# One buffer for the outer weights of both halves of a convolution, filled pair by pair from DRAM in each half image

## The chip, the core and the metric

The kernel runs on one core of a Trainium2 chip. The time is the device time of one execution in microseconds (us); the number compared is the median of the runs. The core has a matrix engine (TensorE, PE in the profile), a vector engine (VectorE, DVE), a scalar engine (ScalarE, ACT), a general engine (GpSimd, POOL) and a sync engine (SyncE, SP), which here only issues transfers. All five run their own instruction streams and meet at semaphores. Sixteen DMA engines move data between DRAM and the on-chip memory; SP, ACT and POOL each have a queue to them.

## What is computed

The reference takes `x` of shape (32, 256, 28, 28) in float32, averages it over 12 log-polar bins of a 9x9 window, convolves the 12 averages with `w_conv1` (256x256x4x3), adds a 1x1 convolution and a bias, normalises each channel over the whole batch, adds `x`, and clips at zero:

```
xp = log_pooling(x)                              # 12 bin averages for each pixel
out = conv(xp, w_conv1, stride=(4, 3)) + conv(x, w_center) + b_center
out = (out - mean) * rsqrt(var + EPS)            # mean, var over batch, height, width
out = out * gamma + beta
return relu(out + x)
```

The batch statistics need every image before the first output can be written, so the work has two phases.

## The kernel before, in words

**Phase 1** goes over 32 images, and in each over the two halves `c` of the 256 input channels, 128 channels a half. A half image has the number `s = 2 * image + c`, 0 to 63. For each half image VectorE builds sums and differences of shifted copies of `x` (helped by two accumulating transfers a half from POOL, `row2`, which the profile calls `row`, and `ends`), ScalarE and VectorE split them into a high and a low part (`inner_split`, `pooled_split`), and TensorE multiplies them with weights that are split in the same way: three matmuls (lines 888 to 890) for each product. The weights have 16 taps. Ten are inner taps (`w_first` for half 0, `w_inner` for half 1); six are outer taps, `w_first_outer` for half 0 and `w_outer` for half 1, each 128 x 3072 float32. The outer taps are used in three pairs `j`, 24 matmuls each; the inner part of a half image is 60 matmuls. TensorE adds to `pooled_done` after each pair (line 946) and to `inner_done` after the inner part (line 929).

**The order on SP** (`image_steps`, line 382) is one load of `x` for each half image, for the next image, which waits for three sums of VectorE and ScalarE, and one store of the previous image's result `y` to `y_dram` for each image.

**Phase 2**, called the tail here, reads `y` and `x` of all 32 images again, scales and clips them and writes the output. It uses the memory of phase 1 as 31 places of 784 KB (1568 columns); place `k` holds the `y` (even `k`) or the `x` (odd `k`) of the tail's image slots 1 to 15. Most places are filled while phase 1 is still running, as soon as what lay there has been used for the last time. SP fills place 1 before the next to last image's steps, and places 2 to 8 behind them, with `load_places(2, 9)`. Then come (lines 427 to 441) `load_places(9, AFTER_STAGE)` with `AFTER_STAGE` 10, `load_places(AFTER_STAGE, AFTER_FIRST_INNER)` with 13 after the last but one half image's inner part, `load_places(AFTER_FIRST_INNER, AFTER_FIRST)` with 15 after its third pair, and the rest as the last half image goes on. Sixteen images are in flight at a time, two rounds in all; in the second round every load waits for a store of the first.

Of the kernel before, what the change touches and what calls it, by code (L numbers as in the profile page):

```python
# [6 lines left out]

def conv_bn_relu_program(nc, x, x_wide, w_raw, w_side, b_center, gamma, beta, out, y_dram):
    F32 = mybir.dt.float32
    F32R = mybir.dt.float32r  # L10
# [9 lines left out]
    CHANNELS = P * CH  # L20
# [50 lines left out]
    with ctx:  # L71
# [11 lines left out]
        with ExitStack() as phase1:  # L83
            def reused(name, size, dt=F32):
                size = -(-size // 8) * 8
                start_of[name] = used[0]
                used[0] += size
                end_of[name] = used[0]
                return phase1.enter_context(nc.sbuf_tensor(name, [P, size], dt))

            w_stage = reused("w_stage", CH * RAW * CHANNELS)

            spare = reused("spare", 10 * CH * HW - CH * RAW * CHANNELS)
            w_first = reused("w_first", 2 * INNER_TAPS * CHANNELS, F32R)
            w_first_outer = reused("w_first_outer", 2 * (TAPS - INNER_TAPS) * CHANNELS, F32R)

            d03 = reused("d03", ROW3_H * (W + 3) + EDGES)
            row2 = reused("row2", (W + 3) * ROW2_H)
            ends = reused("ends", W * ENDS_H)
            INNER = 6 * HALF  # L100
            inner_split = reused("inner_split", 2 * INNER, F32R)
            w_inner = reused("w_inner", 2 * INNER_TAPS * CHANNELS, F32R)
            pooled_split = reused("pooled_split", PAIRS * 2 * PAIR, F32R)
            w_outer = reused("w_outer", 2 * (TAPS - INNER_TAPS) * CHANNELS, F32R)

# [33 lines left out]

        def w_part(c, lo, tap):  # L140

            if tap < INNER_TAPS:
                return (w_first, w_inner)[c], (lo * INNER_TAPS + tap) * CHANNELS
            return (w_first_outer, w_outer)[c], (lo * (TAPS - INNER_TAPS) + tap - INNER_TAPS) * CHANNELS

# [10 lines left out]
        def outer_weights(c, g):  # L156

            a, b = (t - INNER_TAPS for t in GROUPS[g][:2])
            n = (1, (b - a) * CHANNELS)
            split = (w_first_outer, w_outer)[c]  # L160
            return (view(split, a * CHANNELS, n),
                    view(split, (TAPS - INNER_TAPS + a) * CHANNELS, n),
                    view(spare, ((25, 6)[c] + a) * CHANNELS, n))
# [14 lines left out]

        AFTER_STAGE = places_within("spare")
        AFTER_FIRST_INNER = places_within("w_first")  # L180
        AFTER_FIRST = places_within("w_first_outer")
        AFTER_SUMS = places_within("ends")
# [49 lines left out]
        w_hi_ready = sem("w_hi_ready")  # L232
        w_lo_ready = sem("w_lo_ready")
        w_outer_hi_ready = sem("w_outer_hi_ready")
        w_outer_begun = sem("w_outer_begun")
# [132 lines left out]
        def _(sp):  # L368
# [10 lines left out]

            def image_steps(image, first=False, last=False):  # L380
# [71 lines left out]
        def _(act):  # L452
            def split_weights(c, groups):
                for g in groups:
                    a, b, raw, factor = GROUPS[g]
                    if raw is None:
                        act.wait_ge(w_sums_ready, c + 1)
                        source = w_sums(c, 0, b - a)
                    else:
                        act.wait_ge(w_loaded[c][raw >= RAW_OUTER], 16)  # L460
                        source = view(w_stage, (c * RAW + raw) * CHANNELS, (1, (b - a) * CHANNELS))
                    dst, at = w_part(c, 0, a)
                    nc.scalar.activation(view(dst, at, (1, (b - a) * CHANNELS)), source, ACT.Copy,
                                         scale=factor).then_inc(w_hi_ready, 1)
# [159 lines left out]
        def _(dve):  # L624
# [36 lines left out]
            def lo_of_weights(c, groups):  # L661
                for g in groups:
                    a, b, raw, factor = GROUPS[g]
                    dve.wait_ge(w_hi_ready, c * (len(GROUPS) - 1) + g + 1)
                    if raw is None:
                        source = w_sums(c, 0, b - a)
                    else:
                        source = view(w_stage, (c * RAW + raw) * CHANNELS, (1, (b - a) * CHANNELS))
                    hi, hi_at = w_part(c, 0, a)
                    lo, lo_at = w_part(c, 1, a)  # L670
# [210 lines left out]
        def _(pe):  # L881
            def products(c, o, tap, place, buf, hi, lo, *dims, start=False, stop=False):

                hi_w, hi_at = w_part(c, 0, tap)
                lo_w, lo_at = w_part(c, 1, tap)
# [12 lines left out]

            with pe.Fori(0, IMAGES) as image:
                for c in range(CH):  # L900
                    s = CH * image + c
                    pe.wait_ge(w_lo_ready, c * (len(GROUPS) - 1) + M_GROUP)
                    pe.wait_ge(inner_lo_ready, 2 * s + 1)
# [12 lines left out]
                    if c == CH - 1:  # L916
                        last.then_inc(m_done, 1)
                    pe.wait_ge(w_lo_ready, c * (len(GROUPS) - 1) + INNER_GROUPS)
                    pe.wait_ge(inner_lo_ready, 2 * s + 2)
# [10 lines left out]
                    for j in range(PAIRS):  # L930
                        if c == j == 0:
                            pe.wait_ge(w_lo_ready, FIRST_OUTER_GROUP)
                        elif j < 2:
                            pe.wait_ge(w_outer_lo_ready[2 * c + j - 1], 16)
                        pe.wait_ge(pooled_lo_ready, PAIRS * s + j + 1)
                        u, h = PAIR_SHAPE[j]
                        for m, (u0, h0) in enumerate(PAIR_PLACES[j]):
                            for o in range(CH):
                                for q in range(2):
                                    place = view(acc, (2 * o + q) * BANK + u0 * H + h0, (H, u), (1, h))  # L940

                                    between, step = (HALF_PLANE, h) if j == 2 else (h, 2 * h)
                                    at = 2 * j * PAIR + m * PAIR // 2 + q * between
                                    last = products(c, o, TAP_OUTER + 2 * j + m, place, pooled_split, at, at + PAIR,
                                                    (step, u), (1, h), stop=c == CH - 1 and j == PAIRS - 1 and m == 1)
                        last.then_inc(pooled_done, 1)


# [46 lines left out]
```

## Time and profile before

| | us |
|---|---|
| median of 3 runs | 1601.26 (1601.02 to 1601.95) |
| the profiled execution's own time | 1600.99 |
| its span | 1599.3 |
| PE busy | 1456.9 |
| DVE busy | 1467.5 |
| ACT busy | 770.1 |
| POOL busy | 129.5 |

The span is what the profiler records, from the first to the last instruction; 1.7 us of the execution's time lie around it. TensorE works from the start to 1460.7 us, and the tail takes the rest. DVE's sum is the larger one because DVE works in the tail too.

### The profile page before, as it was taken

To read this page: it belongs to the slowest core of one execution; us is meant where nothing else is said; L and a number is where in the kernel's file an instruction comes from. 1 tells how busy PE (TensorE), PEld (TensorE's weight loads), DVE (VectorE), ACT (ScalarE), POOL (GpSimd) and SP (SyncE) were. 2 spreads that over 40 slices of the span, in tenths; PEclk is the share of its full clock that TensorE was granted. 3 is DMA by queue.
4 is the path that set the end of the run, shared out by engine and by line. 5 is a ranking of instruction groups with operands and counts; after the bars stand their busy time and mean duration, and the time that the engine had idled before them with its cause. 6 is when DMAs were issued, how large, how long until landed. Compare 5 with 4: busy or idle time off the path is not lost.

```text
span 1599.3 us, 22801 instructions
## 1 busy us (share of the span) xinstructions
PE 1456.9 (91%) x8518; PEld 1455.7 (91%) x8518; DVE 1467.5 (92%) x1500; ACT 770.1 (48%) x863; POOL 129.5 (8%) x165
## 2 busy tenths in 40 slices
PE   9999999999999999999999999999999999995000
PEld 9999999999999999999999999999999999995000
DVE  8999999999999999999999999999999999996731
ACT  6554454544444454445444554445444554444632
POOL 2100000000000000000000000000000000000100
PEclk9999999999999999999999999999999999998555
DMA  8544444334434444344434444344434444569999
GB/s 219 100 120 91 74 85 94 77 85 90 88 77 86 74 85 91 76 89 86 88 77 90 74 85 87 78 92 85 86 78 86 81 85 105 161 193 383 416 425 402
DMA packets 47721, 201.65 MB, mean 126 GB/s; under 512 B 5664, under 2 KB 5664, under 8 KB 47712
## 3 DMA queue, kind: packets, MB, share of 16 engines
q0 software_dynamic: 21824, 86.55, 29.9%
q1 hardware_dynamic: 21024, 89.32, 15.4%
q10 hardware_dynamic: 4864, 25.69, 3.9%
q14 instruction: 7, 0.06, 0.0%
q8 instruction: 2, 0.03, 0.0%
HBM read 148.85 MB, written 49.77 MB: 124 GB/s over the span
## 4 chain that ended last, share of the span: by engine, by line
PE 88%; ACT 4%; ACTq 3%; DVE 3%; issue 1%; DMA 0%; DVEq 0%
PE acc L888 29%; PE acc L890 29%; PE acc L889 29%; ACTq L620 3%; ACT phase L617 2%; ACT phase_rest L617 2%; DVE phase_rest L625 1%; DVE pooled_split L626 0%; ACT unread L554 0%; DVE d L625 0%; ACT x_pad L617 0%; DVE inner_split L626 0%; DMA x_pad<-x 0%; DVE w_first L671 0%; DVE w_inner L671 0%
## 5 line engine op out<-in xcount | busy, mean ns | idle before, releaser
L501 ACT ACTIVATE pooled_split<-phase_rest 128x1456 fp32r<-128x1456 f32 x192 | 273.7, 1425 | 581.0 <-DVE phase_rest L625 581.0
L626 DVE TENSOR_TENSOR pooled_split<-phase_rest,pooled_split 128x1456 fp32r<-128x1456 f32 x192 | 318.0, 1671 | 0.0
L888 PE MATMUL acc<-pooled_split,w_first_outer 128*128 128x364 f32 x768 | 253.7, 330 | 0.3 <-DVE pooled_split L626 0.3
L888 PE MATMUL acc<-pooled_split,w_outer 128*128 128x364 f32 x768 | 252.1, 328 | 0.8 <-DVE pooled_split L626 0.8
L890 PE MATMUL acc<-pooled_split,w_outer 128*128 128x364 f32 x768 | 252.8, 329 | 0.0
L889 PE MATMUL acc<-pooled_split,w_outer 128*128 128x364 f32 x768 | 252.5, 329 | 0.0
L889 PE MATMUL acc<-pooled_split,w_first_outer 128*128 128x364 f32 x768 | 252.5, 329 | 0.0
L890 PE MATMUL acc<-pooled_split,w_first_outer 128*128 128x364 f32 x768 | 252.3, 329 | 0.0
L888 PE MATMUL acc<-inner_split,w_inner 128*128 128x392 f32 (+1 forms) x640 | 215.8, 337 | 1.3 <-DVE w_inner L671 1.3
L888 PE MATMUL acc<-inner_split,w_first 128*128 128x392 f32 (+1 forms) x640 | 216.7, 339 | 0.0
L889 PE MATMUL acc<-inner_split,w_inner 128*128 128x392 f32 (+1 forms) x640 | 216.6, 338 | 0.0
L890 PE MATMUL acc<-inner_split,w_inner 128*128 128x392 f32 (+1 forms) x640 | 216.6, 338 | 0.0
L890 PE MATMUL acc<-inner_split,w_first 128*128 128x392 f32 (+1 forms) x640 | 215.9, 337 | 0.0
L889 PE MATMUL acc<-inner_split,w_first 128*128 128x392 f32 (+1 forms) x640 | 215.4, 337 | 0.0
L480 ACT ACTIVATE inner_split<-phase_rest 128x1568 fp32r<-128x1568 f32 x64 | 97.5, 1524 | 127.5 <-DVE phase_rest L625 127.5
L888 PEld LDWEIGHTS acc<-pooled_split,w_outer 128*128 128x128 f32 x768 | 144.2, 188 | 1.1 <-DVE pooled_split L626 1.1
L888 PEld LDWEIGHTS acc<-pooled_split,w_first_outer 128*128 128x128 f32 x768 | 144.4, 188 | 0.6 <-DVE pooled_split L626 0.6
L889 PEld LDWEIGHTS acc<-pooled_split,w_outer 128*128 128x128 f32 x768 | 144.5, 188 | 0.0
L889 PEld LDWEIGHTS acc<-pooled_split,w_first_outer 128*128 128x128 f32 x768 | 144.5, 188 | 0.0
L890 PEld LDWEIGHTS acc<-pooled_split,w_first_outer 128*128 128x128 f32 x768 | 144.4, 188 | 0.0
L890 PEld LDWEIGHTS acc<-pooled_split,w_outer 128*128 128x128 f32 x768 | 144.4, 188 | 0.0
L305 POOL DMA_DIRECT2D row<-x_wide x64 | 56.2, 878 | 1039.3 <-ACT row L490 1019.0
(110 smaller groups left out, 2493.2 us busy)
## 6 DMA issues: line engine op xcount, KB each, us to landing
row<-x_wide POOLq DMA_DIRECT2D x64, 558.0 KB, 5.8
ends<-x_wide POOLq DMA_DIRECT2D x64, 504.0 KB, 5.5
x_pad<-x SPq DMA_DIRECT2D x64, 392.0 KB, 3.1
y_dram<-y_stage SPq DMA_DIRECT2D x30, 784.0 KB, 3.3
out<-phase ACTq DMA_DIRECT2D x16, 784.0 KB, 28.2
phase<-y_dram SPq DMA_DIRECT2D x15, 784.0 KB, 15.3
phase_rest<-y_dram SPq DMA_DIRECT2D x14, 784.0 KB, 13.4
out<-phase_rest ACTq DMA_DIRECT2D x14, 784.0 KB, 29.8
```

Source lines behind the costliest of these rows:

```text
L305: return pool.dma_start(view(buf, 0, (1, n_columns * TALL_PITCH)), x_wide[bass.ds(image, 1), :, c, bass.ds((first_column + EDGE) * TALL_PI ...
L480: nc.scalar.activation(view(inner_split, 0, (1, SD)), reused_view(INNER_LOW, (1, SD)), ACT.Copy)\
L501: nc.scalar.activation(view(pooled_split, 2 * j * PAIR, (1, PAIR)), reused_view(POOLED_LOW + 2 * j * PAIR, (1, PAIR)), ACT.Copy)\
L617: nc.scalar.activation(x_slot(d, o), x_slot(d, o), ACT.Relu, bias=bn_shift[:, o:o + 1]).then_inc(relu_done, 1)
L620: act.dma_start(out[tail_image(round_, d)].rearrange("p c w h -> p c (w h)"), x_slot_whole(d)).then_inc(stored[d], 16)
L625: add = lambda out_, a, b: nc.vector.tensor_tensor(out_, a, b, ALU.add)
L626: sub = lambda out_, a, b: nc.vector.tensor_tensor(out_, a, b, ALU.subtract)
L888: nc.tensor.matmul(place, hi_w, hi_in, start=start, stop=False)
L889: nc.tensor.matmul(place, lo_w, hi_in, start=False, stop=False)
L890: return nc.tensor.matmul(place, hi_w, lo_in, start=False, stop=stop)
```

## The change

The two buffers for the outer weights become one, `w_outer`. Half 0's outer weights are made in it; half 1's are made in a new buffer `w_made` that lies ahead of `w_first` in memory and is used by image 0 alone. Once both are made, SP stores them to a new DRAM tensor `w_dram`. From half image 3 on, each pair's weights (both parts, 128 x 2 x 512 float32, 512 KB) are loaded into their third of `w_outer` when the same pair of the half image before is done. TensorE's first image is written out ahead of its loop, since it reads other buffers.

```
-            w_first_outer = reused("w_first_outer", 2 * (TAPS - INNER_TAPS) * CHANNELS, F32R)
+            spare = reused("spare", 12 * CH * HW - CH * RAW * CHANNELS - 2 * (TAPS - INNER_TAPS) * CHANNELS)
+            w_made = reused("w_made", 2 * (TAPS - INNER_TAPS) * CHANNELS, F32R)
...
-        AFTER_STAGE = places_within("spare")
+        AFTER_STAGE = places_within("w_made")
         AFTER_FIRST_INNER = places_within("w_first")
-        AFTER_FIRST = places_within("w_first_outer")
...
+            def save_outer_weights():
+                sp.wait_ge(w_lo_ready, FIRST_OUTER_GROUP)
+                sp.wait_ge(w_outer_lo_ready[0], 16)
+                for c in range(CH):
+                    if c == 1:
+                        for k in range(1, 3):
+                            sp.wait_ge(w_outer_lo_ready[k], 16)
...
+                    sp.dma_start(w_dram[c].rearrange("p l f -> p (l f)"), ...).then_inc(w_saved, 16)
+                sp.wait_ge(w_saved, CH * 16)
+
+            def load_outer_weights(s, c, j):
+                sp.wait_ge(pooled_done, PAIRS * s - PAIRS + j + 1)
+                dst, src = outer_of_pair(c, j)
+                sp.dma_start(dst, src).then_inc(w_outer_loaded[j], 16)
...
+                    change = not first and not (second and c == 0)
+                    if change:
+                        load_outer_weights(s, c, 0)
+                        load_outer_weights(s, c, 1)
                     if not last:
                         sp.wait_ge(row3_ready, CH * image + c + 1)
                         sp.wait_ge(v_ready, CH * image + c + 1)
                         sp.wait_ge(ends_begun, CH * image + c + 1)
                         load_x(image + 1, c)
+                    if change:
+                        load_outer_weights(s, c, 2)
                     if c == 0 and not first and not last:
+                        if second:
+                            sp.wait_ge(first_added, 32)
                         sp.wait_ge(y_ready, CH * image + FREE)
...
             image_steps(0, first=True)
-            sp.wait_ge(first_added, 32)
-            with sp.Fori(1, LAST - 2) as image:
+            save_outer_weights()
+            image_steps(1, second=True)
+            with sp.Fori(2, LAST - 2) as image:
                 image_steps(image)
...
             sp.wait_ge(inner_done, CH * IMAGES - 1)
             load_places(AFTER_STAGE, AFTER_FIRST_INNER)
-            sp.wait_ge(pooled_done, PAIRS * (CH * IMAGES - 1))
-            load_places(AFTER_FIRST_INNER, AFTER_FIRST)
             sp.wait_ge(inner_lo_ready, 2 * CH * IMAGES)
             sp.wait_ge(pooled_ready, PAIRS * CH * IMAGES)
-            load_places(AFTER_FIRST, AFTER_SUMS)
+            load_places(AFTER_FIRST_INNER, AFTER_SUMS)
...
-            with pe.Fori(0, IMAGES) as image:
+            def image_steps(image, first=False):
                 for c in range(CH):
                     s = CH * image + c
-                    pe.wait_ge(w_lo_ready, c * (len(GROUPS) - 1) + M_GROUP)
+                    if first:
+                        pe.wait_ge(w_lo_ready, c * (len(GROUPS) - 1) + M_GROUP)
...
                     for j in range(PAIRS):
-                        if c == j == 0:
+                        if not first:
+                            pe.wait_ge(w_outer_loaded[j], 16 * (s - 1))
+                        elif c == j == 0:
                             pe.wait_ge(w_lo_ready, FIRST_OUTER_GROUP)
...
+            image_steps(0, first=True)
+            for j in range(PAIRS):
+                pe.sem_inc(w_outer_loaded[j], 16)
+            with pe.Fori(1, IMAGES) as image:
+                image_steps(image)
```

SP's queue in the main loop, half 0 of an image, before: the load of `x` behind its three waits, and the store of `y`.

```order
13 L370 ISA [waits ends_begun,v_ready,row3_ready]
14 L370 DMA x_pad<-x 128x784
15 L389 ISA [waits y_ready]
16 L389 DMA y_dram<-y_stage 128x1568
17 L383 REGISTER_ALU
```

The same place now:

```order
20 L408 DMA w_outer<-w_dram 128x2x512 [waits pooled_done]
21 L406 REGISTER_ALU
22 L408 DMA w_outer<-w_dram 128x2x512 [waits pooled_done]
23 L419 REGISTER_ALU
24 L376 ISA [waits ends_begun,v_ready,row3_ready]
25 L376 DMA x_pad<-x 128x784
26 L408 DMA w_outer<-w_dram 128x2x512 [waits pooled_done]
27 L429 ISA [waits y_ready]
28 L429 DMA y_dram<-y_stage 128x1568
```

Two loads of weights, each behind a count of TensorE's pairs, have come ahead of the load of `x`, and a third between it and the store of `y`.

SP's queue at the end of phase 1, before, from place 8 on (`phase` is the memory of the tail's first places; `y_dram` rows fill even places, `x` rows odd ones):

```order
35 L393 DMA phase<-y_dram 128x1568
36 L396 DMA phase<-x 128x1568 [waits y_saved]
37 L393 DMA phase<-y_dram 128x1568 [waits inner_done]
38 L396 DMA phase<-x 128x1568
39 L393 DMA phase<-y_dram 128x1568
40 L396 DMA phase<-x 128x1568 [waits pooled_done]
41 L393 DMA phase<-y_dram 128x1568
42 L396 DMA phase<-x 128x1568 [waits pooled_ready,inner_lo_ready]
```

The same place now, from place 8 on:

```order
60 L433 DMA phase2<-y_dram 128x1568
61 L408 DMA w_outer<-w_dram 128x2x512 [waits pooled_done] x6
62 L436 DMA phase2<-x 128x1568 [waits y_saved]
63 L433 DMA phase2<-y_dram 128x1568
64 L436 DMA phase2<-x 128x1568
65 L433 DMA phase2<-y_dram 128x1568 [waits inner_done]
66 L436 DMA phase2<-x 128x1568
67 L433 DMA phase2<-y_dram 128x1568
68 L436 DMA phase2<-x 128x1568 [waits pooled_ready,inner_lo_ready]
```

Six loads of weights, those of the last two half images, now stand between place 8 and place 9 (row 62). Places 9, 10 and 11 have no wait of TensorE's own any more, 12, 13 and 14 wait for `inner_done`, and all of them come behind row 61.

## Rows read from the trace of the kernel before

**Rows 1.** The page: busy time by engine, and the DMA rate in 40 slices.

```profile
PE 1456.9 (91%) x8518; PEld 1455.7 (91%) x8518; DVE 1467.5 (92%) x1500; ACT 770.1 (48%) x863; POOL 129.5 (8%) x165
...
GB/s 219 100 120 91 74 85 94 77 85 90 88 77 86 74 85 91 76 89 86 88 77 90 74 85 87 78 92 85 86 78 86 81 85 105 161 193 383 416 425 402
```

**Rows 2.** Windows of three half images: stretch, busy by engine, clock, DMA share, GB/s.

```profile
51.34:73.88 22.54, 22.54 (x132) 22.54 (x133) 20.81 (x22) 13.22 (x14) 4.13 (x5) 1.00 0.50 89
795.01:817.55 22.54, 22.54 (x133) 22.54 (x133) 22.02 (x22) 13.64 (x18) 2.60 (x3) 1.00 0.42 78
1426.10:1448.65 22.55, 22.55 (x134) 22.55 (x133) 22.37 (x22) 11.93 (x15) 0.87 (x1) 1.00 0.83 265
```

**Rows 3.** PE in order of time around 795 us: start, duration, instruction.

```profile
794.83 0.34 PE L890 MATMUL acc<-inner_split,w_first 128*128 128x392 f32 x1
795.01 0.33 PE L888 MATMUL acc<-pooled_split,w_first_outer 128*128 128x364 f32 x1
...
807.01 0.34 PE L888 MATMUL acc<-inner_split,w_inner 128*128 128x392 f32 x1
...
817.57 0.33 PE L888 MATMUL acc<-pooled_split,w_outer 128*128 128x364 f32 x1
```

**Rows 4.** SP in order of time, 795 to 845 us.

```profile
803.34 22.96 SPq L370 DMA_DIRECT2D x_pad<-x  x2
831.77 0.36 SPq L389 DMA_DIRECT2D y_dram<-y_stage  x1
```

**Rows 5.** The page's DMA issues: count, size of one, median us to landing.

```profile
row<-x_wide POOLq DMA_DIRECT2D x64, 558.0 KB, 5.8
...
x_pad<-x SPq DMA_DIRECT2D x64, 392.0 KB, 3.1
```

**Rows 6.** DMA issues from 1389 to 1412 us.

```profile
row<-x_wide POOLq DMA_DIRECT2D x1, 558.0 KB, 9.6
```

**Rows 7.** POOL in order of time: a start transfer, two in phase 1.

```profile
42.48 0.87 POOL L339 DMA_DIRECT2D w_outer<-spare  x1 [9.47 <-ACT w_outer L476]
...
836.52 0.87 POOL L305 DMA_DIRECT2D row<-x_wide  x1 [19.63 <-ACT row L490]
...
1397.48 0.87 POOL L305 DMA_DIRECT2D row<-x_wide  x1 [14.80 <-ACT row L490]
```

**Rows 8.** DVE in order of time: the first readers of those two sums.

```profile
847.25 0.97 DVE L625 TENSOR_TENSOR d<-row,x_pad 128x840 f32<-128x840 f32 x1
...
1410.69 0.97 DVE L625 TENSOR_TENSOR d<-row,x_pad 128x840 f32<-128x840 f32 x1
```

**Rows 9.** SP in order of time at the end of phase 1.

```profile
1392.84 0.45 SPq L396 DMA_DIRECT2D phase<-x  x1
1426.13 0.33 SPq L393 DMA_DIRECT2D phase<-y_dram  x1
...
1427.09 0.46 SPq L393 DMA_DIRECT2D phase<-y_dram  x1
1438.13 0.33 SPq L396 DMA_DIRECT2D phase<-x  x1
...
1448.70 0.33 SPq L396 DMA_DIRECT2D phase_rest<-x  x1
```

**Rows 10.** Windows from the end of phase 1 to the tail.

```profile
1415.00:1422.00 7.00, 7.00 (x42) 7.00 (x41) 6.45 (x6) 2.77 (x3) 0.00 (x0) 1.00 0.00 0
1439.00:1440.00 1.00, 1.00 (x7) 1.00 (x7) 1.00 (x2) 0.77 (x1) 0.00 (x0) 1.00 0.82 107
1439.00:1460.70 21.70, 21.63 (x127) 21.34 (x126) 10.08 (x10) 5.71 (x5) 0.00 (x0) 1.00 0.92 345
1455.00:1460.00 5.00, 5.00 (x33) 5.00 (x32) 0.00 (x0) 0.00 (x0) 0.00 (x0) 1.00 1.01 424
...
1472.00:1490.00 18.00, 0.00 (x0) 0.00 (x0) 18.00 (x21) 14.02 (x17) 2.38 (x4) 0.50 1.02 403
1490.00:1580.00 90.00, 0.00 (x0) 0.00 (x0) 40.89 (x43) 40.98 (x47) 6.37 (x12) 0.50 1.02 425
```

More of the change, by code:

```diff
@@ L5, with conv_bn_relu_program @@
 from concourse import mybir
-def conv_bn_relu_program(nc, x, x_wide, w_raw, w_side, b_center, gamma, beta, out, y_dram):
+def conv_bn_relu_program(nc, x, x_wide, w_raw, w_side, b_center, gamma, beta, out, y_dram, w_dram):
     F32 = mybir.dt.float32
@@ L91, in conv_bn_relu_program @@
             w_stage = reused("w_stage", CH * RAW * CHANNELS)
-            spare = reused("spare", 10 * CH * HW - CH * RAW * CHANNELS)
+            spare = reused("spare", 12 * CH * HW - CH * RAW * CHANNELS - 2 * (TAPS - INNER_TAPS) * CHANNELS)
+            w_made = reused("w_made", 2 * (TAPS - INNER_TAPS) * CHANNELS, F32R)
             w_first = reused("w_first", 2 * INNER_TAPS * CHANNELS, F32R)
-            w_first_outer = reused("w_first_outer", 2 * (TAPS - INNER_TAPS) * CHANNELS, F32R)
             d03 = reused("d03", ROW3_H * (W + 3) + EDGES)
@@ L138, in row3v_edges, with w_part @@
             return row3v(-ROW3V_AT, (ROW3V_H, W + 3), (1, EDGES))
-        def w_part(c, lo, tap):
+        OUTER_TAPS = TAPS - INNER_TAPS
+        def w_part(c, lo, tap, made=False):
             if tap < INNER_TAPS:
                 return (w_first, w_inner)[c], (lo * INNER_TAPS + tap) * CHANNELS
-            return (w_first_outer, w_outer)[c], (lo * (TAPS - INNER_TAPS) + tap - INNER_TAPS) * CHANNELS
+            at = (lo * OUTER_TAPS + tap - INNER_TAPS) * CHANNELS
+            if made and c == 1:
+                return w_made, at
+            return w_outer, at
         def w_sums(c, first, n):
@@ L159, in outer_weights @@
             n = (1, (b - a) * CHANNELS)
-            split = (w_first_outer, w_outer)[c]
-            return (view(split, a * CHANNELS, n),
-                    view(split, (TAPS - INNER_TAPS + a) * CHANNELS, n),
+            (high, high_at), (low, low_at) = (w_part(c, lo, a + INNER_TAPS, made=True) for lo in range(2))
+            return (view(high, high_at, n), view(low, low_at, n),
                     view(spare, ((25, 6)[c] + a) * CHANNELS, n))
@@ L233, in conv_bn_relu_program @@
         w_lo_ready = sem("w_lo_ready")
+        w_saved = sem("w_saved")
+        w_outer_loaded = [sem(f"w_outer_loaded{j}") for j in range(PAIRS)]
         w_outer_hi_ready = sem("w_outer_hi_ready")
@@ L378, in load_weights, with outer_of_pair, image_steps @@
                     .then_inc(w_loaded[c][part], 16)
-            def image_steps(image, first=False, last=False):
-                for c in range(CH):
+            def outer_of_pair(c, j):
+                n = 2 * CHANNELS
+                return (view(w_outer, j * n, (OUTER_TAPS * CHANNELS, 2), (1, n)).bitcast(F32),
+                        w_dram[c, :, :, j * n:(j + 1) * n])
+            def save_outer_weights():
+                sp.wait_ge(w_lo_ready, FIRST_OUTER_GROUP)
+                sp.wait_ge(w_outer_lo_ready[0], 16)
+                for c in range(CH):
+                    if c == 1:
+                        for k in range(1, 3):
+                            sp.wait_ge(w_outer_lo_ready[k], 16)
+                    made, made_at = w_part(c, 0, INNER_TAPS, made=True)
+                    sp.dma_start(w_dram[c].rearrange("p l f -> p (l f)"),
+                                 view(made, made_at, (1, 2 * OUTER_TAPS * CHANNELS)).bitcast(F32)).then_inc(w_saved, 16)
+                sp.wait_ge(w_saved, CH * 16)
[3 more added lines that the diff above has]
+                sp.dma_start(dst, src).then_inc(w_outer_loaded[j], 16)
+            def image_steps(image, first=False, second=False, last=False):
+                for c in range(CH):
+                    s = CH * image + c
+                    change = not first and not (second and c == 0)
+                    if change:
+                        load_outer_weights(s, c, 0)
+                        load_outer_weights(s, c, 1)
                     if not last:
@@ L461, in split_weights @@
                         source = view(w_stage, (c * RAW + raw) * CHANNELS, (1, (b - a) * CHANNELS))
-                    dst, at = w_part(c, 0, a)
+                    dst, at = w_part(c, 0, a, made=True)
                     nc.scalar.activation(view(dst, at, (1, (b - a) * CHANNELS)), source, ACT.Copy,
@@ L668, in lo_of_weights @@
                         source = view(w_stage, (c * RAW + raw) * CHANNELS, (1, (b - a) * CHANNELS))
-                    hi, hi_at = w_part(c, 0, a)
-                    lo, lo_at = w_part(c, 1, a)
+                    hi, hi_at = w_part(c, 0, a, made=True)
+                    lo, lo_at = w_part(c, 1, a, made=True)
                     nc.vector.scalar_tensor_tensor(
@@ L881, in _, with products @@
         def _(pe):
-            def products(c, o, tap, place, buf, hi, lo, *dims, start=False, stop=False):
-                hi_w, hi_at = w_part(c, 0, tap)
-                lo_w, lo_at = w_part(c, 1, tap)
+            def products(c, o, tap, place, buf, hi, lo, *dims, start=False, stop=False, made=False):
+                hi_w, hi_at = w_part(c, 0, tap, made)
+                lo_w, lo_at = w_part(c, 1, tap, made)
                 hi_w, lo_w = (view(w, at + o * P, (1, P)) for w, at in ((hi_w, hi_at), (lo_w, lo_at)))
@@ L917, in _ @@
                         last.then_inc(m_done, 1)
-                    pe.wait_ge(w_lo_ready, c * (len(GROUPS) - 1) + INNER_GROUPS)
+                    if first:
+                        pe.wait_ge(w_lo_ready, c * (len(GROUPS) - 1) + INNER_GROUPS)
                     pe.wait_ge(inner_lo_ready, 2 * s + 2)
@@ L944, in _ @@
                                     last = products(c, o, TAP_OUTER + 2 * j + m, place, pooled_split, at, at + PAIR,
-                                                    (step, u), (1, h), stop=c == CH - 1 and j == PAIRS - 1 and m == 1)
+                                                    (step, u), (1, h), stop=c == CH - 1 and j == PAIRS - 1 and m == 1,
+                                                    made=first)
                         last.then_inc(pooled_done, 1)
+            image_steps(0, first=True)
[3 more added lines that the diff above has]
+                image_steps(image)
 def kernel(x, L0_conv_w_conv1, L0_conv_w_center, L0_conv_b_center, L0_conv_gamma, L0_conv_beta):
@@ L990 @@
     y_dram = nc.dram_tensor("y_dram", (images, 128, halves * height * width), f32, kind="Internal").ap()
-    conv_bn_relu_program(nc, *args, out, y_dram)
+    w_dram = nc.dram_tensor("w_dram", (halves, 128, 2, 6 * channels), f32, kind="Internal").ap()
+    conv_bn_relu_program(nc, *args, out, y_dram, w_dram)
     result = run_bass_kernel_spmd(nc, [arrays], core_ids=[0])
```

## The prediction, made before the changed kernel was run

> **What bounds the kernel now.** I read the page's busy shares first, then windows of single half images, then the engines in order of time, and last windows of the end. The page shows TensorE busy for 91% of the span and the DMA rate at 74 to 120 GB/s until late, then near 400 [rows 1]. The windows make two regimes of it. In phase 1 TensorE has no gap: a half image takes 22.54 us, and TensorE is busy for all 22.54 of them at full clock, from 51.34 us on [rows 2]. VectorE is busy for 22.02 of a middle half image, so it has 0.5 us to spare. From 1460.70 us TensorE has nothing to do, and the DMA engines are busy all the time, at 425 GB/s from 1490 to 1580 us [rows 10]. So phase 1 is bound by TensorE and the tail by the bytes that have not been moved when it begins. A change counts if it opens a gap on TensorE, or if it changes how many bytes are still to be moved.
>
> **Part 1, the memory.** Does one buffer less make room? No. Before, the 1568-column places are cut from 48,632 columns: stage and spare 15,680, `w_first` 5120, `w_first_outer` 3072, the three sum buffers 3128, `inner_split` 4704, `w_inner` 5120, `pooled_split` 8736, `w_outer` 3072. Now stage, spare and `w_made` take 18,816 and the rest 29,880, in all 48,696. Both give 31 places. The tail has the same 16 slots, two rounds and bytes. What moves is when a place is free: `AFTER_STAGE` goes from 10 to 12, `AFTER_FIRST_INNER` from 13 to 15.
>
> **Part 2, the reloads in phase 1.** Half images 3 to 63 load three pairs each, 183 loads of 0.524 MB, 95.9 MB. Per half image that is 1.57 MB, or 70 GB/s over 22.54 us, on top of 78 [rows 2]; together 148 against the 424 that pure loads reach [rows 10].
>
> Is a reload in time? The pairs run from 795.01 to 807.01 us, so one takes 4.0 us, and the next half image's pair 0 starts at 817.57 [rows 3]. Pair 0's third is free at 799.0 and wanted at 817.57, which leaves 18.6 us; the other two pairs have the same. No trace row shows a 512 KB reload. The nearest are the 392 KB load of `x` with 3.1 us and, as the slow end, a 558 KB accumulating transfer under a full queue with 9.6 us [rows 5, 6]. I take 3.5 us, by the nearer one; even 9.6 is 9 us below what there is. Cost 0.
>
> Does SP get to them? It now waits for pair 1 before the load of `x`. Pair 1 ends at 803.0, the load of `x` goes out at 803.34 anyway, and the second one at 803.34 + 22.96, that is 826.3, behind the pair 1 that ends at 817.57 + 8 = 825.6 [rows 3, 4]. What is queued behind the wait is delayed by a DMA issue of some 0.4 us, and that `x` is read only in the next image's sums. Pair 2's load follows at 807.0 and 829.6, the store of `y` at 831.77 as before. Cost 0.
>
> Do the loads slow others? The tightest neighbour is `row`, the accumulating sum. It is issued at 836.52, lands 5.8 us later, and VectorE reads it at 847.25, so 4.9 us are spare [rows 5, 7, 8]. The reloads would go out near 821.6, 825.6, 829.6 and 844.2, none within those 5.8 us. `ends` has more room. Under a full queue `row` took 9.6 us, from 1397.48 to 1407.1, and was read at 1410.69 with no wait [rows 6 to 8]. And TensorE ran a half image in 22.55 us with the DMA engines 83% busy [rows 2]. Cost 0; if the cover is gone, see the third rival.
>
> TensorE's own waits: leaving out the waits for results, a half image had four waits for weights against constants (two of them in the inner part), now three against a register, one ahead of each pair. The step into pair 0, with two waits, costs 795.01 - 794.83 = 0.18 us from start to start, and the mean step of the inner part is (817.57 - 807.01) / 60 = 0.176 us, so a wait that is already met is worth next to nothing [rows 3]. Bounds: 0.01 us a half image either way, 0.6 us in all. I take 0.
>
> **Part 3, the start.** Two stores of 1.57 MB (3.7 us each at 425 GB/s) leave SP from 43 us on, behind the load of `x` for image 1. The low outer weights, issued at 42.48 [rows 7], share the engines with the first. They are wanted by pair 1 of half image 1, at 51.34 + 4 = 55.3 us [rows 2]. With the 5.8 to 9.6 us of the other accumulating transfers, from 43.35 on, they land by 53.0. The second store ends near 58, and SP's next item, the load of `x` for image 2, waits for VectorE's half image 2 beyond 60 us; it used to wait for `first_added` too and now goes earlier. TensorE's first image moved out of the loop adds one entry to a loop. Cost 0, at most 1 us.
>
> **Part 4, the end of phase 1.** Here SP's order bites. Place 9 used to be issued at 1392.84 and 10 to 12 from 1426.13 to 1427.09; 13 and 14 waited for the last but one half image's pair 2 at 1438.13 [rows 9]. Now six reloads stand ahead of place 9, and the last of them waits for that same pair 2. So places 9 to 12 are issued at 1438.1 or later. That is 4 x 0.803 = 3.21 MB that the DMA engines had moved by then, partly before a stretch in which they did nothing: 0 GB/s from 1415 to 1422 us [rows 10]. The last reload, 0.524 MB, falls there too. Together 3.735 MB more to move from 1438 us on, at 425 GB/s 8.8 us.
>
> Part of it fits into gaps. From 1439 to 1460.7 the engines moved 345 x 21.7 = 7.49 MB, which is 17.6 us of work at 425 GB/s [rows 10]; 4.1 us were lost to waits for places and to the starts of transfers. With 17 loads in line from 1439 on, only the first start stays, 0.75 us (107 GB/s in the first microsecond). That gives back 3.3 us. Between 1460.7 and the end the engines are full, so what is left over moves the end one for one:
>
> 8.8 - 3.3 = +5.5 us.
>
> Bounds: if only the gaps in the busy share can be filled (8% of 21.7 us, less 0.2), 1.6 us come back and +7.2 stays; if all 4.1 come back and the stretch from 1472 to 1490 us at 403 GB/s takes up its 0.9 us as well, +3.7 [rows 10]. I take +5.5, since the starts lie beside other transfers once the queue is long.
>
> The Trainium skill, page "DMA: Bandwidth & Descriptors", section "Where 436 GB/s comes from", says that the DRAM side binds at about 358 GB/s for transfers between it and on-chip memory. By that the 3.735 MB would cost 10.4 us instead of 8.8, and the sum would be near +7. That lies inside the forecast's bounds below, so it is no case of its own. This trace disagrees: loads alone, before any store of the tail, ran at 424 GB/s [rows 10].
>
> **The sum.** 0 + 0 + 0 + 5.5 on the profiled execution's own 1600.99 us gives 1606.5. The median of the runs is 0.27 us above that execution, which I leave within the rounding.
>
> **Rivals.**
> 1. The later places cost nothing, because the tail has room that the profile hides. For it: ACT and DVE pace the first slots, and the rate is 403 there. Against it: the busy share is 1.02 throughout, and the regained 0.9 us are counted. With a slack of 3 us or more it gives 1601 to 1604.
> 2. Not slower: the two waits that leave the inner part let TensorE close up. If they had cost 0.1 us a half image between them, 62 half images would give 6.2 us, and 1606.5 becomes 1600.3. It decides from 5.5 / 62 = 0.09 us a half image on, half a matmul's step. For it: a half image has one wait less. Against it: a step with two waits takes 0.18 us, the mean one 0.176 [rows 3].
> 3. Contention: if the reloads double `row`'s landing to 11.6 us in every half image, it is 0.9 us late in the tight half of each image; VectorE's spare 0.5 covers some, and 0.4 x 30 = 12 us come on top: 1618.5. It decides from a landing of 5.8 + 4.9 + 0.5 = 11.2 us on. Against it: 9.6 us with the queue full throughout [rows 6].
> 4. The reloads are not hidden. If each half image's first one kept TensorE 0.5 us, 61 of them would cost 30 us: 1637. It takes a landing of over 18 us. That the change does not do what it says, room for more tail places, is no rival but counted in part 1.
>
> **How the numbers follow.** Forecast 0.80; rival 1 0.09; rival 2 0.02; rival 3 0.05, rival 4 0.01; the rest, a steady cost of 1 to 3 us, 0.03. The forecast's own bounds are 1604.7 to 1608.2; a pair load of two 2 KB pieces per partition at half rate adds 1.2, the start at most 1, TensorE's steps 0.6 either way. So the range is 1603.9 to 1610.5. Faster or slower by 0.2% (3.2 us, about what a measurement of this kernel can tell from no change) begins at 1598.1 and 1604.5. Slower has the forecast, rivals 3 and 4 and the rest, 0.89, less 0.01 at the lower edge, 0.88; same has rival 1 and that edge, 0.10; faster 0.02.
>
> **What would show it.** Phase 1's half images stay at 22.54 us with TensorE full, and TensorE ends at 1460.7, give or take 1. The middle slices of the DMA rate rise from 85 to about 155 GB/s. SP issues the last reload and then places 9 to 14 in a row just after 1438.1; from 1440 the rate stays near 425; the tail from TensorE's end is 5 to 6 us longer. The forecast is wrong if TensorE shows gaps before pairs, if `row` lands past VectorE's need, or if the tail keeps its length.

## The result, and the profile after

The changed kernel takes 1604.98 us (median of 13 runs) against 1601.26 us before: ratio 1.0022, 95% interval 1.0015 to 1.0030. That is 3.7 us slower, inside the stated range of 1603.9 to 1610.5 and 1.5 us below the forecast of 1606.5. One of the 13 runs took 8371.75 us, and one of the 11 of e1 below 1908.78 us; both are left out of the comparisons, and nothing here explains them. The profiled execution took 1604.98 us with a span of 1603.3 us.

The page of the changed kernel, busy time by engine and the DMA rate in 40 slices, beside [rows 1]:

```profile
PE 1456.1 (91%) x8518; PEld 1455.0 (91%) x8518; DVE 1467.5 (92%) x1500; ACT 768.8 (48%) x863; POOL 129.5 (8%) x165
...
GB/s 219 188 192 166 141 148 160 160 159 151 150 155 159 141 148 160 160 159 156 150 150 159 147 143 159 160 159 159 150 149 157 151 140 178 215 229 423 425 425 405
```

TensorE is busy 0.8 us less than before [rows 1], and the middle slices have risen from about 85 to about 155 GB/s, as the added 70 GB/s would have it. Windows of the changed kernel, columns as in [rows 2]:

```profile
795.00:817.50 22.50, 22.50 (x133) 22.50 (x133) 21.78 (x22) 13.12 (x17) 2.60 (x3) 1.00 0.65 147
1438.00:1439.00 1.00, 1.00 (x7) 1.00 (x6) 1.00 (x2) 0.74 (x1) 0.00 (x0) 1.00 0.51 84
1439.00:1440.00 1.00, 1.00 (x8) 1.00 (x7) 1.00 (x2) 0.79 (x2) 0.00 (x0) 1.00 0.86 186
1439.00:1460.70 21.70, 20.62 (x122) 20.32 (x120) 10.12 (x10) 4.99 (x6) 0.00 (x0) 1.00 1.01 415
1472.00:1490.00 18.00, 0.00 (x0) 0.00 (x0) 18.00 (x20) 14.32 (x17) 1.77 (x3) 0.50 1.02 422
1490.00:1580.00 90.00, 0.00 (x0) 0.00 (x0) 39.95 (x41) 36.17 (x41) 6.96 (x14) 0.50 1.02 425
```

Phase 1 is as full of TensorE as before, with the DMA share at 0.65 where it was 0.42. At its end the DMA rate is 415 GB/s where it was 345 [rows 10], so the gaps there are nearly closed. From 1472 to 1490 us it is 422 where it was 403 [rows 10], at the same share of 1.02. Most of that difference lies in five microseconds; the kernel before, then the changed one:

```profile
1480.00:1485.00 5.00, 0.00 (x0) 0.00 (x0) 5.00 (x6) 3.85 (x5) 1.10 (x2) 0.50 1.02 371
```

```profile
1480.00:1485.00 5.00, 0.00 (x0) 0.00 (x0) 5.00 (x6) 3.76 (x5) 0.75 (x1) 0.50 1.02 419
```

TensorE of the changed kernel in order of time: the first matmul of each part of two half images, and the last of all.

```profile
794.50 0.33 PE L927 MATMUL acc<-pooled_split,w_outer 128*128 128x364 f32 x1
...
806.47 0.33 PE L927 MATMUL acc<-inner_split,w_inner 128*128 128x392 f32 x1
...
817.03 0.33 PE L927 MATMUL acc<-pooled_split,w_outer 128*128 128x364 f32 x1
...
829.00 0.34 PE L927 MATMUL acc<-inner_split,w_first 128*128 128x392 f32 x1
...
1459.30 0.32 PE L929 MATMUL acc<-pooled_split,w_outer 128*128 128x364 f32 x1
```

Half 0's three pairs take 806.47 - 794.50 = 11.97 us where they took 12.00 [rows 3]; half 1's take 11.97 in both. Worked out in the same way over the complete half images from 75 to 1440 us, the means are 12.003 and 11.971 us before (half 0, half 1), 11.967 and 11.971 now. The mean inner parts are unchanged within 0.01 us. So TensorE ends at 1459.6 us, 1.0 us sooner than before.

The reloads and their neighbours on the page of the changed kernel (columns as in [rows 5]):

```profile
w_outer<-w_dram SPq DMA_DIRECT2D x183, 512.0 KB, 4.0
row<-x_wide POOLq DMA_DIRECT2D x64, 558.0 KB, 5.8
...
x_pad<-x SPq DMA_DIRECT2D x64, 392.0 KB, 4.2
```

A reload lands in 4.0 us, `row` in the same 5.8 as before, and the load of `x`, which now has pair 1's reload just ahead of it, in 4.2 instead of 3.1. The 4.0 is a median: the reload issued at 1406.66, behind places 2 to 8, took 9.6. From the issues of 1406 to 1407 us:

```profile
w_outer<-w_dram SPq DMA_DIRECT2D x1, 512.0 KB, 9.6
```

SP of the changed kernel at the end of phase 1, beside [rows 9]:

```profile
1406.66 30.98 SPq L408 DMA_DIRECT2D w_outer<-w_dram  x6
1437.69 0.60 SPq L436 DMA_DIRECT2D phase<-x  x1
...
1440.54 0.44 SPq L433 DMA_DIRECT2D phase<-y_dram  x1
1443.12 0.33 SPq L436 DMA_DIRECT2D phase<-x  x1
```

The six reloads come first, the last of them just before 1437.7. Then places 9 to 14 go out in a row up to 1440.5. Place 9 had gone out at 1392.84 [rows 9]. The tail behind TensorE's end is 1603.3 - 1459.6 = 143.7 us; it was 1599.3 - 1460.6 = 138.7.

### The profile page after: what moved, and what is told of

It reads as the page before. It is cut to its first block, busy times and chain, and to the rows that moved or that the text cites. A ratio compares the mean times of both kernels' runs of the same rounds, so it can differ in the third digit from the quotient of the medians.

```text
span 1603.3 us, 23115 instructions
## 1 busy us (share of the span) xinstructions
PE 1456.1 (91%) x8518; PEld 1455.0 (91%) x8518; DVE 1467.5 (92%) x1500; ACT 768.8 (48%) x863; POOL 129.5 (8%) x165
## 4 chain that ended last, share of the span: by engine, by line
PE 88%; ACT 4%; ACTq 4%; DVE 3%; issue 0%; DMA 0%; DVEq 0%
PE acc L929 29%; PE acc L928 29%; PE acc L927 29%; ACTq L659 4%; ACT phase L656 2%; ACT phase_rest L656 2%; DVE phase_rest L664 1%; DVE pooled_split L665 0%; ACT unread L593 0%; DVE d L664 0%; ACT x_pad L656 0%; DVE inner_split L665 0%; DMA x_pad<-x 0%; DVE w_first L710 0%; DVE w_inner L710 0%
## 5 line engine op out<-in xcount | busy, mean ns | idle before, releaser
L929 PE MATMUL acc<-pooled_split,w_outer 128*128 128x364 f32 x1512 | 497.5, 329 | 0.0
L928 PE MATMUL acc<-pooled_split,w_outer 128*128 128x364 f32 x1512 | 497.2, 329 | 0.0
L927 PE MATMUL acc<-pooled_split,w_outer 128*128 128x364 f32 x1512 | 496.1, 328 | 0.0
L928 PEld LDWEIGHTS acc<-pooled_split,w_outer 128*128 128x128 f32 x1512 | 284.5, 188 | 0.0
L929 PEld LDWEIGHTS acc<-pooled_split,w_outer 128*128 128x128 f32 x1512 | 284.2, 188 | 0.0
L927 PEld LDWEIGHTS acc<-pooled_split,w_outer 128*128 128x128 f32 x1512 | 284.0, 188 | 0.2 <-issue 0.2
L664 DVE TENSOR_TENSOR phase_rest<-d 128x784 f32<-128x784 f32 (+1 forms) x128 | 130.3, 1018 | 2.2
L593 ACT ACTIVATE unread<-y_stage,minus_pivot 128x784 f32<-128x784 f32 x124 | 117.1, 944 | 22.5 <-DVE y_stage L664 14.7
L927 PEld LDWEIGHTS acc<-inner_split,w_inner 128*128 128x128 f32 x640 | 120.1, 188 | 1.5 <-DVE w_inner L710 1.5
L929 PEld LDWEIGHTS acc<-inner_split,w_inner 128*128 128x128 f32 x640 | 120.3, 188 | 0.0
L928 PEld LDWEIGHTS acc<-inner_split,w_inner 128*128 128x128 f32 x640 | 120.3, 188 | 0.0
L927 PEld LDWEIGHTS acc<-inner_split,w_first 128*128 128x128 f32 x640 | 120.2, 188 | 0.0
## 6 DMA issues: line engine op xcount, KB each, us to landing
phase<-y_dram SPq DMA_DIRECT2D x15, 784.0 KB, 12.9
phase_rest<-y_dram SPq DMA_DIRECT2D x14, 784.0 KB, 12.9
```

Source lines behind the costliest of these rows:

```text
L593: nc.scalar.activation(unread[:, :], y_place(image, o * HW, (1, HW)), function, bias=minus_pivot[:, o:o + 1], accum_out=sums[:, bass.ds((k ...
L664: add = lambda out_, a, b: nc.vector.tensor_tensor(out_, a, b, ALU.add)
```

## The experiments

Theory 1: the loss is traffic that SP's order pushes into the stretch where the DMA engines are full; the reloads themselves are hidden. The rival: reloads cost what they move, wherever the places are loaded. Theory A: the microsecond that TensorE gains belongs to the place of the weights in memory. The rival: it belongs to half 0, or to the changed waits and loop.

**e1, SP's order mended.** The changed kernel, with

```
             load_places(2, 9)
-            image_steps(LAST, last=True)
             sp.wait_ge(y_saved, 16 * (LAST - 1))
             load_places(9, AFTER_STAGE)
+            for j in range(PAIRS):
+                load_outer_weights(CH * LAST, 0, j)
             sp.wait_ge(inner_done, CH * IMAGES - 1)
             load_places(AFTER_STAGE, AFTER_FIRST_INNER)
+            for j in range(PAIRS):
+                load_outer_weights(CH * LAST + 1, 1, j)
```

> The changed kernel with SP's order mended at the end of phase 1: places 9 to 11 are issued right behind places 2 to 8, then the three weight reloads of half image 62, then (behind inner_done 63) places 12 to 14, then the three reloads of half image 63. All reloads stay. Theory 1 (the loss is the late places, 3.2 MB of traffic pushed into the full stretch; reloads themselves are free): TensorE ends near 1459.7 as in the changed kernel, the tail behind it shrinks from 143.6 to about 138.6 us, total 1600.0 to 1600.9. Rival (the loss is the reload traffic and the weights' DRAM tensor, wherever the places are loaded): stays at 1605.

Measured: 1600.19 us against 1601.29, ratio 0.9993, interval 0.9983 to 1.0002. SP in order of time (place 9, the reloads of half image 62, place 12, the reloads of 63), and windows of the end:

```profile
1396.49 0.48 SPq L436 DMA_DIRECT2D phase<-x  x1
...
1406.82 8.48 SPq L408 DMA_DIRECT2D w_outer<-w_dram  x3
1425.32 0.33 SPq L433 DMA_DIRECT2D phase<-y_dram  x1
...
1429.33 8.47 SPq L408 DMA_DIRECT2D w_outer<-w_dram  x3
```

```profile
1439.00:1460.70 21.70, 20.78 (x122) 20.48 (x121) 10.13 (x9) 5.13 (x5) 0.00 (x0) 1.00 0.80 311
...
1472.00:1490.00 18.00, 0.00 (x0) 0.00 (x0) 18.00 (x20) 14.33 (x17) 2.37 (x4) 0.50 1.02 405
```

All 183 reloads are still there, and the loss is gone. The places are moved earlier, the gaps up to 1460.7 us are back (311 GB/s), and the tail is 138.7 us again. Theory 1 holds, its rival (1605) falls. By its median this version is 1.1 us faster than before, but the interval includes 1.

**e2, the late places alone.** The kernel before, with

```
-            load_places(9, AFTER_STAGE)
-            sp.wait_ge(inner_done, CH * IMAGES - 1)
-            load_places(AFTER_STAGE, AFTER_FIRST_INNER)
             sp.wait_ge(pooled_done, PAIRS * (CH * IMAGES - 1))
-            load_places(AFTER_FIRST_INNER, AFTER_FIRST)
+            load_places(9, AFTER_FIRST)
```

> The kernel before, with one thing of the change alone: places 9 to 12 wait, as 13 and 14 do, for pooled_done 189. No reloads, no buffer change. Theory 1: 3.21 MB more to move from 1438 us on is 7.6 us at 425 GB/s, less 3.6 us of gaps filled up to 1460.7 and 0.8 us from 1472 to 1490: +3.2 us, so 1604.4 (1603.8 to 1605.2), TensorE still ending at 1460.7. Rival (the reloads make the loss): 1601.3.

Measured: 1604.77 us, ratio 1.0021, interval 1.0012 to 1.0030. SP's issue of place 9, and the windows of the end:

```profile
1438.07 0.33 SPq L396 DMA_DIRECT2D phase<-x  x1
```

```profile
1439.00:1460.70 21.70, 21.52 (x127) 21.23 (x125) 10.08 (x10) 5.70 (x5) 0.00 (x0) 1.00 1.00 409
1472.00:1490.00 18.00, 0.00 (x0) 0.00 (x0) 18.00 (x20) 14.08 (x16) 1.85 (x3) 0.50 1.02 415
```

With no reload anywhere, four late places make +3.5 us, nearly all of the loss, by the same marks: 409 and 415 GB/s where the kernel before has 345 and 403 [rows 10].

**e6, the reload traffic taken away.** The changed kernel, each reload 16 columns instead of 512:

```
-                return (view(w_outer, j * n, (OUTER_TAPS * CHANNELS, 2), (1, n)).bitcast(F32),
-                        w_dram[c, :, :, j * n:(j + 1) * n])
+                return (view(w_outer, j * n, (OUTER_TAPS * CHANNELS, 2), (1, 16)).bitcast(F32),
+                        w_dram[c, :, :, j * n:j * n + 16])
```

> The changed kernel with every wait and every reload in place, but a reload moves 16 of its 512 columns (8 KB of floats a part instead of 256 KB), so the products of half images from 3 on use the wrong half's weights for the rest. It takes the reload traffic alone away. Theory 1: phase 1 does not change, TensorE ends at 1459.7; the last reload's 0.524 MB leaves the full stretch, 1.2 us: 1603.7 (1603.3 to 1604.2). Rival (reload traffic is a large part of the loss or hides a gain in phase 1): 1601.5 or less, or TensorE ends earlier than 1459.4.

Measured: 1604.46 us, ratio 1.0020, interval 1.0011 to 1.0029. TensorE ends at 1459.8, so 93 of the 96 MB of reloads less change nothing in phase 1. The whole is 0.5 us shorter than the changed kernel, where I had expected 1.2, and so lies just outside the 1603.3 to 1604.2 that I had given. SP shows why part of the reload's price is not its bytes:

```profile
1437.90 0.60 SPq L436 DMA_DIRECT2D phase<-x  x1
```

Place 9 still goes out behind an issue of the last reload, small as it is, so at 1437.90, only 0.2 us sooner than e2's 1438.07, though TensorE ends 0.7 us sooner (1459.8 against 1460.5).

**e5 and e8, the traffic doubled.** The kernel of e1, with a second transfer of the same size behind every reload, DRAM to DRAM; in e8 only up to half image 57.

```
                 sp.dma_start(dst, src).then_inc(w_outer_loaded[j], 16)
+                if isinstance(s, int) and s > 3:      # e8 alone
+                    return
+                again = PAIRS * (s - 3) + j
+                if not (isinstance(s, int) and again == 0):
+                    sp.wait_ge(loaded_again, 16 * again)
+                sp.dma_start(again_dram[:, :, :], src).then_inc(loaded_again, 16)
```

> The kernel of e1 with a second transfer of the same 512 KB behind every reload, from the DRAM tensor of the weights to another DRAM tensor, ordered behind the one before it. Traffic in phase 1 goes from about 148 to about 218 GB/s. Theory 1 (the reloads are hidden with room to spare): TensorE ends within 0.3 us of 1459.8, row lands in 6 to 8 us (median), total 1600.0 to 1601.5. Rival (contention near its turning point): row lands past 11.2 us in many half images, gaps show on DVE or PE, total above 1605.

Measured for e5: 1610.16 us, ratio 1.0053, interval 1.0037 to 1.0068. My expectation missed. The trace has no gap on TensorE from 80 to 1424 us, and then one. The wait, the windows around it, and the DMA issues from 1398 to 1412 us:

```profile
PE acc L934 <- DMA w_outer<-w_dram: 4.8, 1, 4.8
```

```profile
1424.70:1429.80 5.10, 0.34 (x2) 0.02 (x1) 5.10 (x6) 4.52 (x8) 0.86 (x1) 0.91 1.06 294
1429.80:1432.00 2.20, 2.18 (x7) 2.18 (x8) 1.99 (x2) 2.00 (x5) 0.00 (x0) 0.50 1.08 237
...
1436.00:1440.00 4.00, 4.00 (x26) 4.00 (x25) 2.99 (x5) 0.00 (x0) 0.00 (x0) 1.00 0.86 297
```

```profile
w_outer<-w_dram SPq DMA_DIRECT2D x2, 512.0 KB, 23.2
```

Two reloads, issued behind the ten places 2 to 11 (the second of them behind a second transfer as well), take a median of 23.2 us, more than the 18.6 they have. TensorE waits 5 us and then runs some 5 us more at a granted clock of about 0.5 (1.2 GHz instead of 2.4); it ends at 1467.2. SP itself is held up too:

```profile
1411.60 3.50 SPq L409 DMA_DIRECT2D w_outer<-w_dram  x1
1433.53 0.49 SPq L413 DMA_DIRECT2D again_dram<-w_dram  x1
1434.06 0.61 SPq L409 DMA_DIRECT2D w_outer<-w_dram  x1
```

It stands for some 18 us before the second transfer of 1433.53, which waits until the one issued at 1407.59 has landed, 25.9 us later. So e5 could have shown that doubled traffic costs in itself, or only that it costs among the places, and e8 was made to part these.

> e5 again, but without the second transfers from half image 58 on, so that they never stand among the places of the tail; in the loop the traffic stays doubled (about 218 GB/s). In e5 phase 1 had no gap before 1424 us, then TensorE waited 5.1 us for a reload that stood behind places and second transfers on SP's queue. Theory (traffic was never the matter, only the place in SP's queue was): TensorE ends at 1459.8, the whole takes 1600.2 (1599.6 to 1600.9) as e1 does. Rival (doubled traffic costs by itself): 1602 or more.

Measured for e8: 1600.29 us, ratio 0.9995, interval 0.9985 to 1.0004. Its DMA rate by slices, and its issues:

```profile
GB/s 220 188 262 226 225 221 229 230 222 219 223 232 215 218 220 234 231 223 219 220 230 218 218 217 237 233 217 225 218 232 220 214 216 183 189 349 357 417 425 402
```

```profile
w_outer<-w_dram SPq DMA_DIRECT2D x183, 512.0 KB, 4.2
again_dram<-w_dram SPq DMA_DIRECT2D x165, 512.0 KB, 5.4
row<-x_wide POOLq DMA_DIRECT2D x64, 558.0 KB, 7.5
```

About 225 GB/s all through phase 1, two and a half times the kernel before, cost nothing against e1. `row` lands in 7.5 us instead of 5.8 (the longest in 9.8), still under the 10.7 that it has. What hurt in e5 were the second transfers from half image 58 on. Whether it was their place in SP's queue, SP's wait for each of them, or their bytes in a stretch where the DMA engines were already full, e8 does not show, since it takes away all three.

In e1 the same reloads have the ten places and no second transfers ahead of them. Of its DMA issues from 1406 to 1416 us, and from 1406 to 1407 us alone:

```profile
w_outer<-w_dram SPq DMA_DIRECT2D x3, 512.0 KB, 12.9
```

```profile
w_outer<-w_dram SPq DMA_DIRECT2D x1, 512.0 KB, 15.5
```

The median is 12.9 and the first takes 15.5 of 18.6 us: hidden, but with 3 us to spare. The Trainium skill, page "DMA: Bandwidth & Descriptors", section "Queues, rings and completion order", says that each DMA engine takes the descriptors of one issuing engine's ring in their order. By that a reload waits for all places issued ahead of it. The traces agree: the first reload behind the places took 9.6 us with seven of them ahead (the changed kernel) and 15.5 with ten (e1), which is 5.9 us more, and three places of 0.803 MB at 425 GB/s are 5.7 us. In e5 the reload issued at 1406.58 took 23.1 us with the same ten ahead; the last of these went out at 1401.12 there and at 1397.50 in e1, which leaves about 4 us that the places ahead do not account for.

**e3, e4 and e7, the place of the outer weights.** e3 is the kernel before with the two outer buffers exchanged:

```
-            return (w_first_outer, w_outer)[c], (lo * (TAPS - INNER_TAPS) + tap - INNER_TAPS) * CHANNELS
+            return (w_outer, w_first_outer)[c], (lo * (TAPS - INNER_TAPS) + tap - INNER_TAPS) * CHANNELS
```

> The kernel before with the memory positions of the two outer weight buffers exchanged: half 0 uses the one at the end, half 1 the one behind w_first (places 13 to 15 are loaded last for that reason, so its total time is some us longer and is not the question). In the kernel before, half 0's three pairs take 12.004 us and half 1's 11.971 on average; in the changed kernel both take 11.97. Theory A (the place of the weights in memory costs 0.033 us a half image): the slow one becomes half 1, about 12.00, and half 0 drops to 11.97. Theory B (it belongs to half 0, its waits or neighbours in the loop): half 0 stays at 12.00.

TensorE of e3 in order of time, the starts of the parts:

```profile
795.21 0.33 PE L887 MATMUL acc<-pooled_split,w_outer 128*128 128x364 f32 x1
...
807.18 0.33 PE L887 MATMUL acc<-inner_split,w_inner 128*128 128x392 f32 x1
...
817.73 0.33 PE L887 MATMUL acc<-pooled_split,w_first_outer 128*128 128x364 f32 x1
...
829.73 0.34 PE L887 MATMUL acc<-inner_split,w_first 128*128 128x392 f32 x1
```

Half 0 now takes 11.97 us and half 1 12.00 (means 11.968 and 12.002): the slowness has gone with the place. But the inner part with `w_first`, which did not move, went from a mean of 10.531 us to 10.555, so TensorE ends at 1461.0, 0.4 us later than before. The one run took 1606.29 us; its places 13 to 15 are late, as the expectation says.

e4 is the kernel before with `pad = reused("pad", 64)` ahead of `w_first_outer`.

> The kernel before with 64 unused columns (256 bytes a partition) ahead of w_first_outer, so that it and all later buffers lie 64 columns further. Theory A1 (the place matters by its distance to the data read or its alignment in small steps): half 0's pairs change from 12.004, to 11.97 or higher. Theory A2 (only the coarse region matters) or B: stays at 12.00 and 11.97. Total time within 1 us of 1601.3.

Means 12.003 and 11.971: 64 columns do not matter. Its one run took 1600.36 us, though TensorE ends at 1460.5, where it ended at 1460.6 in the kernel before. A single run can thus lie 0.9 us under the median with nothing gained on TensorE.

e7 is the changed kernel with `w_outer` behind `w_first`, where `w_first_outer` had been, and `w_made` at the end:

```
-            w_made = reused("w_made", 2 * (TAPS - INNER_TAPS) * CHANNELS, F32R)
             w_first = reused("w_first", 2 * INNER_TAPS * CHANNELS, F32R)
+            w_outer = reused("w_outer", 2 * (TAPS - INNER_TAPS) * CHANNELS, F32R)
...
-            w_outer = reused("w_outer", 2 * (TAPS - INNER_TAPS) * CHANNELS, F32R)
+            w_made = reused("w_made", 2 * (TAPS - INNER_TAPS) * CHANNELS, F32R)
```

> The changed kernel with w_outer where w_first_outer lay before (behind w_first, column 20,800) and w_made at the end; places 13 to 15 are loaded last, so the total time is some us longer and is not the question. Theory A (the place in memory sets it): the three pairs take 12.00 us in both halves, TensorE ends near 1459.7 + 2.0 = 1461.7. Theory C (the gain came from the reloads, the written-out first image or the changed waits): pairs stay at 11.97 and TensorE ends near 1459.7.

TensorE of e7, the starts of the parts and the end:

```profile
795.69 0.33 PE L927 MATMUL acc<-pooled_split,w_outer 128*128 128x364 f32 x1
...
807.69 0.34 PE L927 MATMUL acc<-inner_split,w_inner 128*128 128x392 f32 x1
...
818.25 0.33 PE L927 MATMUL acc<-pooled_split,w_outer 128*128 128x364 f32 x1
...
830.25 0.34 PE L927 MATMUL acc<-inner_split,w_first 128*128 128x392 f32 x1
...
1461.68 0.32 PE L929 MATMUL acc<-pooled_split,w_outer 128*128 128x364 f32 x1
```

12.00 us in both halves, and TensorE ends 2.4 us later than in the changed kernel (one run, 1607.82 us in all). Of these 2.4, the pairs make (12.003 + 12.002 - 11.967 - 11.971) x 31 = 2.1, and the inner parts (10.560 + 10.548 - 10.558 - 10.537) x 31 = 0.4. Theory A holds in both directions for the pairs; reloads, waits and the written-out image are all there in e7 and gain nothing.

## Why the prediction was right, point by point

**The two regimes, and the memory.** Right. The tail has the same bytes and slots, and e1 has the reloads without the loss. The forecast's mechanism held; 1604.98 lies near the lower end of its own bounds, 1604.7 to 1608.2, because one term was mis-sized, as the part on the end of phase 1 shows. The range around them was not quite the sum of its parts: these give 1604.7 - 0.6 = 1604.1 and 1608.2 + 1.2 + 1 + 0.6 = 1611.0, not 1603.9 and 1610.5.

**The reloads in phase 1 at cost 0.** Right, with room: e6 takes them away and e8 doubles their traffic, and TensorE ends between 1459.6 and 1459.8 us each time. The landing was put at 3.5 us and is 4.0, of 18.6. `row` did not move. The third rival's turning point, 11.2 us, was not reached even in e8 (median 7.5, longest 9.8). The fourth rival, a late reload, came true in e5 alone, and by a way that I had not named: places, and second transfers, around it in the queue, not its own length.

**The start at cost 0.** Right. Pair 0 of half image 1 begins at 51.34 us in both traces, and the pairs of half image 2 at 73.94 before and 73.97 now.

**TensorE's waits.** The sum had 0 with 0.6 us either way. TensorE gained 1.0 us, and not by its waits, as the second rival had it, but by the place of the buffer (e3, e7). That term was missing. It also brought the total less than it brought TensorE: from 1438 us on the DMA engines are the bound, and place 9 goes out at 1437.69 where it would have been at 1438.1, 0.4 us sooner and not 1.0. Whether the full microsecond arrives where the DMA engines have gaps is not shown. In e1 and e8 it looks so (1600.19 against 1601.29, 1600.29 against 1601.35), but both intervals include 1, and e4's one run was as fast with no gain on TensorE.

**The end of phase 1.** The mechanism was right, place by place; the size was too large. The step was "8.8 - 3.3 = +5.5 us". The four places alone cost 3.5 us (e2), where the same working gives 7.6 - 3.3 = 4.3. What failed is the 3.3 us regained. Up to 1460.7 us the regained rate is (415 - 345) x 21.7 / 425 = 3.6 us, from 1438 to 1439 another 84 x 1 / 425 = 0.2 us, and from 1472 to 1490 another (422 - 403) x 18 / 425 = 0.8 us. Together that is 4.6, and 8.8 - 4.6 = 4.2 stands beside the 4.0 by which the profiled execution is longer (1604.98 against 1600.99). For e2 the same windows give 7.6 - 3.3 - (415 - 403) x 18 / 425 = 3.8, against 3.7 (1604.72). I had put the 0.8 only at the lower bound, taking the rate of 403 for a property of that stretch. It is not one. In the traces whose end of phase 1 is as before or as in e1 it is 401 to 410 (403, e1 405, e4 410, e8 401), and in those with places 9 to 12 late 415 to 422 (e2 and e6 415). Why the longer queue runs faster there, the traces do not show; the share is 1.01 or 1.02 in all of them. The last reload was priced at 0.524 / 0.425 = 1.2 us and costs 0.5 (e6 against the changed kernel): its bytes partly move before the stretch is full (84 GB/s from 1438 to 1439, where e6 has 16 and the kernel before nothing). Together: +3.5 by the places (e2), -0.3 from e2 to e6, which has the earlier TensorE and six small issues, +0.5 by the last reload's bytes, +3.7 in all.

**The first rival**, that the tail has room which the profile hides, got 0.09, and a quarter of it was true, if the 0.8 us are taken as such room: it needed 3.

What stays open: why 72 matmuls with weights at column 20,800 take 0.033 us longer than at 45,560, and why the inner part behind them changes too (e3). Only these two regions and a shift by 64 columns were tried. Open too are what the second transfers of e5 cost by their place and what by their bytes, and why the tail's rate from 1472 to 1490 us rises with the longer queue.

## What to carry to other kernels

When transfers are added to a queue that issues in program order, price what stands behind them at the ends of the loop, not only the bytes: 96 MB of hidden reloads cost nothing, and four prefetches that ended up behind the last of them cost 3.5 us. To price bytes pushed into a full stretch, first count every microsecond there whose rate is below the best one, even where the busy share says 1.0: here a longer queue filled much of it. And look whether the engine that gets faster is still the bound at that point: the microsecond that TensorE gained brought place 9 forward by 0.4 us only.

## What was not expected of the hardware

The place of a weight buffer in on-chip memory changes the pace of the matmuls that read it: 12.00 us for 72 at column 20,800 of the phase 1 memory, 11.97 at column 45,560 and beyond, and it follows the buffer when the halves are exchanged (e3) and when both halves use it (e7). It is 0.3%, and here 1 us. The inner part that follows is touched as well: with `w_first` in its place it took 10.531 us before and 10.555 in e3.

The rate of transfers with the share of the engines at 1.02 was 403 GB/s in one trace and 422 in another over the same stretch, and 371 and 419 from 1480 to 1485 us. A busy share of 1 in this profile is thus not the full rate.
